# Attention with a fused output convolution: the work on the last chunk's keys and queries is moved between engines, and four places of the order are changed

## What is computed

```python
q = jnp.einsum('oc,bcn->bon', Wq, xf) + bq[None, :, None]   # 32 channels
k = jnp.einsum('oc,bcn->bon', Wk, xf) + bk[None, :, None]   # 32 channels
v = jnp.einsum('oc,bcn->bon', Wv, xf) + bv[None, :, None]   # 256 channels
att = jnp.einsum('bdi,bdj->bij', q, k) / jnp.sqrt(jnp.asarray(d_k, x.dtype))
att = jax.nn.softmax(att, axis=-1)
out = gamma * jnp.einsum('bcj,bij->bci', v, att).reshape(b, c, h, w)
cat = jnp.concatenate([out, x], axis=1)
fused = jnp.einsum('oc,bchw->bohw', Wf, cat) + bf[None, :, None, None]
```

## Time and profile before

| | |
|---|---|
| median of 3 runs | 1968.14 us (1967.75 to 1968.16) |
| profiled execution: its own time | 1968.11 us |
| its span in the trace | 1966.3 us |
| TensorE (PE) busy | 1947.5 us |
| ScalarE (ACT) busy | 1711.4 us |
| VectorE (DVE) busy | 1683.6 us |
| GpSimd (POOL) busy | 1413.3 us |
| granted TensorE clock, mean | 0.997 |

### The profile page before, as it was taken

One profiled execution on the slowest core, in us unless ns is written; L12 is line 12 of the kernel. 1 busy time (PEld: TensorE's weight loads), 2 busy tenths in 40 slices (PEclk: granted clock), 3 DMA queues, 4 the chain that ended last, 5 costly groups with the idle time before them and its releaser, 6 DMA issues.

```text
span 1966.3 us, 46458 instructions
## 1 busy us (share of the span) xinstructions
PE 1947.5 (99%) x15656; PEld 1918.7 (98%) x15656; DVE 1683.6 (86%) x2700; ACT 1711.4 (87%) x2282; POOL 1413.3 (72%) x689
## 2 busy tenths in 40 slices
PE   9999999999999999999999999999999999999999
PEld 8899999999989999999999999999999999999998
DVE  7888989887888889888688888889868888888996
ACT  7899999997789999999788999999978899999996
POOL 3778777778477787777747777777765777777775
PEclk9999999999999999999999999999999999999999
DMA  4311111110321111111042111111104111111111
GB/s 143 85 22 18 16 22 22 21 19 16 124 72 23 20 17 17 22 21 22 12 134 63 23 22 18 17 18 21 22 12 135 38 23 22 21 18 17 19 22 17
DMA packets 297816, 69.70 MB, mean 35 GB/s; under 512 B 280528, under 2 KB 281296, under 8 KB 297680
## 3 DMA queue, kind: packets, MB, share of 16 engines
q1 hardware_dynamic: 296864, 67.90, 16.0%
q10 hardware_dynamic: 816, 0.13, 0.0%
HBM read 34.41 MB, written 33.55 MB: 35 GB/s over the span
## 4 chain that ended last, share of the span: by engine, by line
PE 94%; DVE 2%; POOL 1%; issue 1%; ACT 1%; DVEq 0%; ACTq 0%; POOLq 0%
PE ps_o L429 74%; PE ps_s L421 11%; PE ps_o L293 3%; PE ps_p L293 3%; PE ps_s L310 1%; DVE top L673 1%; PE ps_p L328 1%; PE ps_p L324 1%; POOL kq_rest L919 0%; ACT raw L512 0%; PE ps_s L283 0%; POOL queries L922 0%; DVE top_j L678 0%; DVE raw L714 0%; ACT keys L524 0%
## 5 line engine op out<-in xcount | busy, mean ns | idle before, releaser
L873 POOL TENSOR_TENSOR raw<-raw,top_m 128x1024 f32<-128x1024 f32 x508 | 1208.6, 2412 | 261.6 <-DVE top_m L708 243.7
L719 DVE TENSOR_TENSOR lo<-ps_p,hi 128x1024 fp32r<-128x1024 f32 x512 | 622.8, 1216 | 158.3 <-ACT ps_p L600 151.7
L673 DVE TENSOR_TENSOR top<-ps_s,top 128x512 f32<-128x512 f32 x960 | 659.0, 686 | 65.8 <-ACT raw L512 12.1
L429 PE MATMUL ps_o<-val_hi,hi 128*128 128x258 f32 x4096 | 663.2, 283 | 7.7 <-DVE val_lo L787 7.7
L593 ACT ACTIVATE hi<-raw 128x1024 fp32r<-128x1024 f32 x508 | 539.7, 1062 | 148.1 <-PE ps_o L429 138.9
L429 PE MATMUL ps_o<-val_lo,hi 128*128 128x256 f32 x4096 | 655.7, 282 | 0.0
L429 PE MATMUL ps_o<-val_hi,lo 128*128 128x258 f32 x4096 | 599.5, 284 | 0.4 <-DVE lo L719 0.4
L512 ACT ACTIVATE raw<-ps_s 128x512 f32<-128x512 f32 x1024 | 553.2, 592 | 33.3 <-DVE top L673 5.4
L429 PEld LDWEIGHTS ps_o<-val_hi,hi 128*128 128x128 f32 x4096 | 565.4, 190 | 8.8 <-DVE val_lo L787 6.2
L429 PEld LDWEIGHTS ps_o<-val_lo,hi 128*128 128x128 f32 x4096 | 563.0, 190 | 0.0
L429 PEld LDWEIGHTS ps_o<-val_hi,lo 128*128 128x128 f32 x4096 | 539.3, 190 | 1.1 <-DVE lo L719 0.8
(11 more groups left out here) (76 smaller groups left out, 1104.2 us busy)
## 6 DMA issues: line engine op xcount, KB each, us to landing
xf<-x SPq DMA_DIRECT2D x32, 512.0 KB, 3.7
conv_d<-conv_st SPq DMA_DIRECT2D x64, 256.0 KB, 2.0
result<-conv_d SPq DMA_DIRECT2D x512, 32.0 KB, 1.8
out<-result SPq DMA_DIRECT2D x510, 32.0 KB, 1.6
raw<-wf2T SPq DMA_DIRECT2D x1, 256.0 KB, 4.1
raw<-wv SPq DMA_DIRECT2D x1, 256.0 KB, 3.9
raw<-wf1T SPq DMA_DIRECT2D x1, 256.0 KB, 4.8
raw<-wkqT ACTq DMA_DIRECT2D x1, 64.0 KB, 2.6
```

The source lines that it names most:

```text
L429: last = nc.tensor.matmul(ps_o[:, i, 0:width], p[:, t % 2, jl * I + i * P:jl * I + (i + 1) * P], v[:, j, 0:width], start=opens and jl == 0 ...
L673: nc.vector.tensor_tensor(top[:, new], scores, top[:, new if half else old], ALU.max).then_inc(max_done, 1)
L719: nc.vector.tensor_tensor(lo[:, t % 2], ps_p[:].rearrange("p h n -> p (h n)"), hi[:, t % 2].bitcast(F32), ALU.subtract).then_inc(lo_done, 1)
L873: nc.gpsimd.tensor_tensor(raw[:, slot], raw[:, slot], top_m[:, r].unsqueeze(1).broadcast_to((P, JQ, I)), ALU.subtract).then_inc(sub_done, 1)
```

## The change

- **Chunk 7's keys.** The second copy of the high parts is made by ScalarE right after the first (counted by `k_doubled`), not by GpSimd.
- **Chunk 7's queries.** ScalarE copies them to `q_raw` (`q_keep`) after it has kept the scores of quad 6, not before. GpSimd's four instructions on them are put into the first block of attention (`late_queries`), before the subtraction at t = 3, which is that of quad 5. TensorE's wait for them moves from t = 2 to t = 7.
- **The first quad.** VectorE makes the values' low parts between the two halves of the first quad's subtraction.
- **The start.** Chunk 0 of the input is loaded and split in two halves of 128 channels. VectorE makes the folded weights' low part before chunk 0's queries' low parts, and TensorE waits for that one alone, not for the bias too.

```diff
 # SyncE, start
-            load_x(0, 0)
+            for k in range(KT):
+                sp.dma_start(xf[:, 0, k], x_v[0:1, :, k, 0:W].rearrange("b p n -> p (b n)")).then_inc(x0_loaded[k], 16)
+            sp.sem_inc(x_loaded[0], 16)
...
 # TensorE, project_kq: first half of chunk 0 by x0_hi_half and x0_split
+                        if first and c == 0 and k == 0:
+                            pe.wait_ge(x0_hi_half, 1)
+                        else:
+                            pe.wait_ge(x_hi_done, C + 1)
...
 # TensorE, chunk 7
                     pe.wait_ge(k_out, C + 1)
-                    pe.wait_ge(k_copied, C + 1)
+                    pe.wait_ge(k_doubled, b + 1)
                     early_scores(c)
...
 # TensorE, attend
-                    if first and t == 2:
+                    if first and t == QUADS - 1:
                         pe.wait_ge(q_out, b * CHUNKS + CHUNKS)
                         pe.wait_ge(q_copied, b * CHUNKS + CHUNKS)
...
 # ScalarE, kq_hi and the end of project for chunk 6
+                    if c == CHUNKS - 1:
+                        act.wait_ge(k_hi_done, C + 1)
+                        nc.scalar.activation(keys[CK:2 * CK, span(c)], keys[0:CK, span(c)].bitcast(F32),
+                                             ACT.Copy).then_inc(k_doubled, 1)
+                        return
...
                 if c == CHUNKS - 2:
                     kq_hi(c + 1, C + 1)
                     early_scores(c)
+                    q_keep(c + 1, C + 1)
...
-                    act.wait_ge(wvf_split, 1)
+                    act.wait_ge(bias_done, 1)
...
 # VectorE, setup_values
-                                               ALU.mult, ALU.subtract)
-                nc.vector.scalar_tensor_tensor(bias[:], ps_s[:, 0, 0:KT, 0], gam, bf_c, ALU.mult, ALU.add).then_inc(wvf_split, 1)
+                                               ALU.mult, ALU.subtract).then_inc(wvf_split, 1)
+                nc.vector.scalar_tensor_tensor(bias[:], ps_s[:, 0, 0:KT, 0], gam, bf_c, ALU.mult,
+                                               ALU.add).then_inc(bias_done, 1)
...
 # VectorE, chunk 7
-                    subtract_first(b * BLOCKS)
+                    subtract_first(b * BLOCKS, 0)
                     values_lo(0)
                     values_lo(1)
+                    subtract_first(b * BLOCKS, 1)
                     split_p(b * STEPS, 0)
...
 # VectorE, chunk 0
-                kq_lo(c, C)
+                k_lo(c, C)
+                if start:
+                    setup_values()
+                q_lo(c, C)
                 if c == CHUNKS - 2:
                     split_x(C + 1, c + 1)
-                if start:
-                    setup_values()
...
 # GpSimd, attend; late_queries holds the four instructions that stood in project
+                    if t == 3 and isinstance(n, int) and n == 0:
+                        pool.wait_ge(sub_done, B * QUADS + (t + 2))
+                        late_queries(b, CHUNKS - 1)
+                        pool.wait_ge(q_out, b * CHUNKS + CHUNKS)
                     if t < QUADS - 2:
                         subtract_top(r, slot)
```

More of the change, by code:

```diff
@@ L123, in attention_conv @@
         wkq_split, wf2_split, wvf_split = sem("wkq_split"), sem("wf2_split"), sem("wvf_split")
+        bias_done = sem("bias_done")
         wvf_ready, id_zeroed, id_made, ones_done = sem("wvf_ready"), sem("id_zeroed"), sem("id_made"), sem("ones_done")
+        x0_loaded = [sem(f"x0_loaded{k}") for k in range(KT)]
+        x0_hi_half, x0_split = sem("x0_hi_half"), sem("x0_split")
         x_loaded = [sem(f"x_loaded{i}") for i in range(2)]
@@ L501, in _, with split_first @@
             nc.scalar.activation(wkq_both[:, :, :, 0], wkq_pair, ACT.Copy).then_inc(wkq_hi_done, 1)
+            def split_first():
+                for k in range(KT):
+                    act.wait_ge(x0_loaded[k], 16)
+                    nc.scalar.activation(hi[:, 0, k * W:(k + 1) * W], xf[:, 0, k], ACT.Copy).then_inc(
+                        x0_hi_half if k == 0 else x_hi_done, 1)
             def split_x(b, c):
@@ L529, in kq_hi, with q_keep @@
                     else:
-                        act.wait_ge(q_out, C)
-                        nc.scalar.activation(q_raw[2 * CK:P], ps_p[2 * CK:P, 0], ACT.Identity,
-                                             bias=bkkqq[2 * CK:P]).then_inc(q_raw_done, 1)
+                        q_keep(c, C)
+                def q_keep(c, C):
+                    act.wait_ge(q_out, C)
+                    nc.scalar.activation(q_raw[2 * CK:P], ps_p[2 * CK:P, 0], ACT.Identity,
+                                         bias=bkkqq[2 * CK:P]).then_inc(q_raw_done, 1)
                 def conv_out(src, ot, C=C):
@@ L564, in project @@
                 if start:
-                    split_x(0, 0)
+                    split_first()
                     act.wait_ge(wf2_loaded, 16)
@@ L660, in split_x, with split_first @@
                                         ALU.subtract).then_inc(x_split, 1)
+            def split_first():
+                for k in range(KT):
+                    dve.wait_ge(x0_hi_half if k == 0 else x_hi_done, 1)
+                    nc.vector.tensor_tensor(lo[:, 0, k * W:(k + 1) * W], xf[:, 0, k], hi[:, 0, k * W:(k + 1) * W].bitcast(F32),
+                                            ALU.subtract).then_inc(x0_split if k == 0 else x_split, 1)
             def fold_scores(base, made, old, new, halves=(0, 1), at_once=False):
@@ L708, in spread_top, with subtract_first @@
                 nc.vector.transpose(top_m[:, r], top_all[:].unsqueeze(2).broadcast_to((P, I // 32, 32))).then_inc(m_done, 1)
-            def subtract_first(B):
+            def subtract_first(B, half):
                 dve.wait_ge(m_done, B + 1)
-                for half, done in enumerate((sub0_half, sub0_done)):
-                    two = raw[:, 0, 2 * half:2 * half + 2]
-                    nc.vector.tensor_tensor(two, two, top_m[:, 0].unsqueeze(1).broadcast_to((P, 2, I)),
-                                            ALU.subtract).then_inc(done, 1)
+                two = raw[:, 0, 2 * half:2 * half + 2]
+                nc.vector.tensor_tensor(two, two, top_m[:, 0].unsqueeze(1).broadcast_to((P, 2, I)),
+                                        ALU.subtract).then_inc(sub0_done if half else sub0_half, 1)
             def split_p(Q, t):
@@ L771, in kq_lo, with q_lo @@
                                             ALU.add).then_inc(k_out, 1)
+                def q_lo(c, C):
                     if c >= LATE:
@@ L894, in project @@
                     pool.wait_ge(x_split, C + 1)
-                pool.wait_ge(k_hi_done, C + 1)
-                pool.sem_inc(kq_seen, 1)
-                nc.gpsimd.tensor_copy(keys[CK:2 * CK, span(c)], keys[0:CK, span(c)]).then_inc(k_copied, 1)
+                if c < CHUNKS - 1:
+                    pool.wait_ge(k_hi_done, C + 1)
+                    pool.sem_inc(kq_seen, 1)
+                    nc.gpsimd.tensor_copy(keys[CK:2 * CK, span(c)], keys[0:CK, span(c)]).then_inc(k_copied, 1)
+                else:
+                    pool.sem_inc(k_copied, 1)
                 if c < LATE:
```

44 lines of the change are left out of this document (26 added, 18 removed).

## The result

The changed kernel takes 1976.70 us (median of 6 runs, 1976.03 to 1977.48) against 1967.92 us before (6 runs, 1966.99 to 1968.16): ratio 1.0047, 95% interval 1.0036 to 1.0057. That is 8.8 us slower, outside the range of 1965.0 to 1974.0. The profiled execution took 1976.7 us, its span is 1974.7, 8.4 more than before, so the two traces hold nearly the whole difference.

A forecast was written before the change was run, and what follows sets the result against it. TensorE was taken as the bound, busy 1947.5 of 1966.3 us. Start -0.73, first image +1.26 and the other three +1.95 gave +2.5 us: 1970.6 us predicted, range 1965.0 to 1974.0.

The forecast's parts named there:

- The step that failed: First block of attention, VectorE's low parts (L719) from step 5 to step 7: claimed to stay 6.98 us, moving as one.
- 38.25: Second image, step 7's `trail` counted from the last matmul of the keys: predicted 38.25 us, against 37.60 before.
- the sum: Whole kernel: start -0.73, first image +1.26, other three images +1.95, together +2.5 us.
- the start: Program start: folded weights' low part made earlier, so TensorE's first values begin 0.73 us earlier; bounds -0.3 to -1.5.
- the hold for the join: Next block's maximum (L678) meeting quad 5's subtraction: at worst 1.21 instead of 0.43 us, covered by VectorE's wait, zero in total.
- The first rival: Late queries' low parts slowed beside VectorE: quad 5 0.88 us later per image, in all +6.0, 1974.1 us; chance 0.16.
- The halves of chunk 0: Start: splitting chunk 0 priced at zero; later loads one issue later, allowed to take up to 0.4 us.
- the forecast's case: The main forecast, 1970.6 us, with late queries and start uncertain: 1968.5 to 1972.0 us; chance 0.60.
- my chain: From GpSimd's first subtraction through late queries, quad 5, ScalarE and VectorE to TensorE's step 7 `trail`: 26.76 us.
- The slow clock of the earlier trace: Second image, TensorE at 1.2 GHz from 560.6 to 563.9: even if kept, step 1 some 1 us later, hidden.
- the queries hidden: Rival: late queries cost nothing in attention because something else waits or GpSimd is in time: -2.4, 1965.7 us; chance 0.16.
- TensorE keep its gain at step 1: Rival: TensorE keeps 1.5 us in each of three images plus the gain at program start: -5.2, 1962.9 us; chance 0.08.

The follow-up runs named there:

- run 1: Changed kernel with one wait added, so GpSimd subtracts quad 7 only after the next block's maximum is spread: 1974.42 us, ratio 1.0035.
- run 3: Changed kernel with chunk 7's late queries moved from before quad 5's subtraction to after quad 7's: 1972.59 us, ratio 1.0026.
- run 4: Kernel before with the late queries alone, put before quad 5's subtraction: 1973.98 us, ratio 1.0033.
- run 11: Changed kernel with the copy of 64 x 8 maxima done by a reduction over one element: 1974.66 us in one run.
- run 6: Changed kernel, first subtraction's halves together, chunk 0 whole, late queries split before quads 5 and 6, quad 7 after the maximum: 1968.42 us, ratio 1.0003.
- run 9: Changed kernel with late queries at the first block's end, first subtraction's halves together, chunk 0 whole: 1968.93 us, ratio 1.0006.
- run 7: Kernel before with the start's new order alone (folded weights' low part first, no wait for the bias), chunk 0 whole: 1966.77 us in one run.
- run 8: Changed kernel with chunk 0 of the input loaded and split as a whole: 1976.57 us in one run.

## Why the prediction was wrong

- **The step that failed** is "VectorE from L719 of step 5 to L719 of step 7: 97.16 - 90.18 = 6.98 ... It moves as one." Measured in the second image: 588.82 - 580.64 = 8.18. Of the 1.20 more, 1.33 - 0.17 = 1.16 are the held copy. I priced that stretch from rows in which no subtraction ran beside the maximum's small instructions, and did not ask where quad 7's subtraction would fall. Runs 1, 3, 4 and 11 show the hold. With 1.16 added, 38.25 becomes 39.41; measured 39.44. Over the four images the held copies make 1.13 + 1.16 + 1.16 + 1.07 = 4.5 us of the 8.2 - 2.5 = 5.7 that the sum fell short, the start 0.4; of the 0.8 left, 0.7 lie in the fourth image, by the third block's start, where TensorE's clock fell (the point on the slow clock below).
- **I asked the right question of the wrong instruction.** I weighed the hold for the join alone and found it covered: it was 0.75 us in the second image (1.39, 0.80 and 0.83 in the others), before a wait of VectorE of 1.28, as I wrote. And I took 0.8 us for the worst; runs 6 and 9 show 2.14 and 2.58 where 0.42 would do, nearly the whole of a subtraction (2.4). The Trainium skill (SBUF — State Buffer, section "SBUF: two separate sides") has the lock held for the whole instruction; the traces agree.
- **The first rival** had the right sign and the right kind, GpSimd and VectorE holding each other, at the wrong place: the queries' own low parts were not slowed (1.28 and 1.29 us). Its ground against, that no VectorE instruction there has both operands in SBUF, held for the queries and not for the subtractions behind them.
- **The start** was mis-sized: -0.73 predicted, 13.04 to 12.76 measured. The order itself gives 0.72, as predicted (run 7). The halves of chunk 0, priced at zero with up to 0.4 us allowed, take about 0.5 back (run 8) by delaying the weights' load. (My bounds for the forecast's case, added up, give 1968.6 to 1972.2, not 1968.5 to 1972.0; nothing hangs on it.)
- **Right:** the first half's subtraction starts 1.34 us earlier (10.13 to 8.79; 1.33 predicted), L714 at 0.42, GpSimd's first subtraction at 11.46 instead of 11.61 (560.06 predicted from 548.57, that is 11.49), ScalarE's step 5 at 578.63 - 550.65 = 27.98, where my chain gives 27.99. The slow clock of the earlier trace rows is gone from this place, and that bought nothing, as said: between 560 and 564 TensorE's mean granted clock, the third number from the end of this row of the windows, is

```profile
560.00:564.00 4.00, 2.92 (x20) 2.51 (x20) 2.38 (x5) 2.61 (x4) 1.89 (x1) 1.00 0.39 139
```

  1.00, full speed (2.4 GHz), yet step 7 comes later.
- **The other rivals** fall: neither were the queries hidden, nor did TensorE keep its gain at step 1. The parts do not add up to the whole: the queries alone cost 6.7 us on the kernel before, undoing them gives 7.7, undoing the split order 4.9 of the same 8.8, because each shifts which instruction meets a subtraction.
- **A slow clock in another place.** In the fourth image of the changed kernel TensorE's granted clock fell to half, 1.2 GHz, from 1567.1 to 1570.5 (1.00 in the kernel before and in the changed kernel's other three images at this step):

```profile
1567.10:1570.50 3.40, 3.40 (x18) 3.40 (x17) 3.11 (x4) 3.28 (x5) 3.40 (x2) 0.50 0.00 0
```

  The third block starts at 69.48 there and at 68.83 in the second image: 0.65 us. Run 8 paid the like in its second image. Ahead of the fall TensorE had waited 0.25, 0.29 and 0.63 us for VectorE, behind the held copy. In the second image waits of 0.36, 0.29 and 0.63 left the clock at full speed; what decides between the two stays open.

## What to carry to other kernels

Before pricing a stretch as one that "moves as one", list VectorE's copies from SBUF to SBUF and its instructions with two operands in SBUF, however small, and lay GpSimd's new timetable beside them: in these traces each that began while a GpSimd instruction ran cost what was left of that one. (Reductions and transposes ran through.) A tuned order has such meetings arranged by tenths of a microsecond, so work that comes earlier can lose its gain one block later; look there for the next meeting, and try a wait that lets the small instruction go first. An experiment on one part should be read by its meetings, not by its sign alone.

## What the runs showed of the hardware

- A join of 128 x 256 (0.42 us alone) that begins beside a GpSimd instruction ends 0.28 to 0.29 us after that one's end, in every case over 0.5 us in the traces of the kernels before and changed and of runs 6 and 9 (19 joins, 0.75 to 2.60 us), and in the 56 such joins of the other traces. Copies of 64 x 8 and 32 x 8 (0.17 and 0.16 alone) end 0.02 to 0.03 us after it; so does the maximum of 64 x 8 with two operands in SBUF (0.16 alone, 1.06 to 1.12 in run 11).
- Not held beside GpSimd: the transposes within VectorE (0.45), reductions (0.40; 0.16 for 64 x 8), and instructions with an operand in PSUM (L709 0.69, L754 1.23).
- It goes the other way as well: the subtraction of GpSimd's that followed right behind the one that had held the join took 2.58 to 2.59 us in the changed kernel's four images, against 2.41, the most frequent length there.
- One load split into two (the same bytes) put those behind it back: `wf1T` was issued 0.4 us later in all traces (3.32 against 2.93) and landed at 7.72 to 8.63 in the six with the split, mean 8.2, against 7.27 to 8.04 in the eleven without, mean 7.6.
- TensorE's granted clock fell to half for 3.4 us in the changed kernel's fourth image and in run 8's second and fourth, behind short waits (0.25 to 0.63 us) that left it at full speed in other images.
